# A decoder in one launch: the scan's C product made in place in SBUF, the state space's kernel spectrum moved to the shared lane, and new orders for all engines

## What is computed

```
x = LN(x + hawk(x))          # RMS norm, gated linear recurrence (RG-LRU), then a gated MLP
x = LN(x + cross_attention)  # 8 heads over a context of 32 positions
x = LN(x + mla + moe)        # latent causal attention, 16 heads; top-2 of 7 experts and a shared one
x = LN(x + selective_scan)   # below
x = LN(x + s4d_block)        # attention over x, FiLM, a state-space convolution by FFT, an MLP
x = LN(x + moe2)             # top-2 of 8 experts and shared ones
```

```
delta = softplus(x Wd + bd);  B = x Wb + bb;  C = x Wc + bc
h[n](t) = exp(delta(t) A[n]) * h[n](t-1) + delta(t) x(t) B[n](t)
y(t) = sum over n of h[n](t) * C[n](t)
```

## Time and profile before

| | us |
|---|---|
| median of 3 runs (lowest, highest) | 494.37 (493.97, 498.09) |
| span of the profiled execution | 494.8 |
| PE busy | 417.6 (84%) |
| DVE busy | 335.1 (68%) |
| ACT busy | 302.1 (61%) |
| POOL busy | 123.7 (25%) |
| 49 table loads on ACT | 62.9 |
| granted PE clock, mean | 0.934 of full speed |

### The profile page before, as it was taken

How to read it: one execution, slowest core, us unless ns; L and a number is a source line. 1 busy time by engine, 2 the same in 40 slices (tenths; PEclk the granted TensorE clock), 3 DMA queues, 4 the chain that set the end, 5 groups by cost and what they waited for, 6 DMA issues and landing times.

```text
span 494.8 us, 5930 instructions
## 1 busy us (share of the span) xinstructions
PE 417.6 (84%) x2049; PEld 203.1 (41%) x2049; DVE 335.1 (68%) x616; ACT 302.1 (61%) x513; POOL 123.7 (25%) x129
## 2 busy tenths in 40 slices
PE   6979868778979999978876874677699899999995
PEld 3535422353335554424332321425466644444442
DVE  2497776488877842745888997998965453554453
ACT  5648795514246679896788885554336687822443
POOL 1100460000420054058729484555020000000000
PEclk9999999959999999989996997668979999999999
DMA  7950000733280000023028778989300000000000
GB/s 266 338 168 15 1 2 0 200 54 148 70 186 5 3 3 1 3 63 108 0 69 208 190 177 229 212 228 273 157 0 1 1 0 1 0 1 0 1 21 21
DMA packets 23613, 42.39 MB, mean 86 GB/s; under 512 B 6965, under 2 KB 12310, under 8 KB 22422
## 3 DMA queue, kind: packets, MB, share of 16 engines
q1 hardware_dynamic: 23476, 41.92, 30.3%
q10 hardware_dynamic: 108, 0.10, 0.1%
HBM read 36.93 MB, written 4.98 MB: 85 GB/s over the span
## 4 chain that ended last, share of the span: by engine, by line
PE 55%; DVE 20%; ACT 8%; POOL 6%; issue 5%; DMA 5%; SPq 0%; DVEq 0%; ACTq 0%; POOLq 0%
DVE AR L1520 7%; PE PS L900 6%; PE PS L927 6%; PE PS L905 6%; ACT AR L1178 5%; PE PS L814 4%; PE PS L828 4%; DVE AR L1841 3%; POOL AR L2158 3%; PE PS L797 3%; PE PS L664 3%; DVE AR L1526 2%; DMA AR<-scan 2%; PE PS L1031 2%; DVE stats L1529 1%
## 5 line engine op out<-in xcount | busy, mean ns | idle before, releaser
L1178 ACT ACTIVATE AR<-PS 128x512 f32<-128x512 f32 (+2 forms) x185 | 98.4, 562 | 99.4 <-PE PS L900 44.2
L1520 DVE TENSOR_TENSOR AR<-PS,AR 128x512 f32<-128x512 f32 (+1 forms) x120 | 79.8, 678 | 57.6 <-PE PS L905 27.7
L2158 POOL TENSOR_TENSOR AR<-AR 128x512 f32<-128x512 f32 (+2 forms) x48 | 53.7, 1129 | 90.9 <-DVE AR L1520 60.0
L1178 ACT ACTIVATE AR<-AR 128x256 f32<-128x256 f32 (+3 forms) x110 | 46.9, 462 | 44.4 <-DVE AR L1520 28.6
L1174 ACT ACT_TABLE_LOAD x49 | 62.9, 1283 | 0.9
L1529 DVE TENSOR_REDUCE stats<-PS 128x1 f32<-128x128 f32 (+4 forms) x88 | 43.6, 525 | 11.5 <-PE PS L800 6.9
L1841 DVE TENSOR_TENSOR_SCAN AR<-PS,AR 128x512 f32<-128x512 f32 x32 | 38.9, 1214 | 2.2 <-ACT PS L1178 2.2
L797 PE MATMUL PS<-RR 97*128 97x512 bf16 (+3 forms) x128 | 31.9, 322 | 6.4 <-DVE stats L1529 3.3
L664 PE MATMUL PS<-AR,W_sq 128*128 128x256 f32 x88 | 26.6, 413 | 12.4 <-ACT AR L1178 7.9
L2244 POOL TENSOR_TENSOR RR<-KL,lags 128x512 f32<-128x512 f32 x24 | 26.6, 1146 | 40.0 <-PE PS L817 39.9
L814 PE MATMUL PS<-RR 100*128 100x512 bf16 (+3 forms) x128 | 29.9, 306 | 1.4 <-ACT AR L1178 1.1
(11 more groups left out here) (239 smaller groups left out, 726.4 us busy)
## 6 DMA issues: line engine op xcount, KB each, us to landing
AR<-scan SPq DMA_DIRECT2D x64, 256.0 KB, 4.1
RR<-in_ffn SPq DMA_DIRECT2D x1, 2688.0 KB, 10.9
RR<-in_ones SPq DMA_DIRECT2D x2, 832.0 KB
RR<-in_ones SPq DMA_DIRECT2D x2, 784.0 KB
RA<-in_moe SPq DMA_DIRECT2D x1, 1539.5 KB, 6.3
W_mla<-in_mla SPq DMA_DIRECT2D x1, 1504.0 KB, 15.4
W_late<-in_late SPq DMA_DIRECT2D x1, 1076.0 KB, 12.0
RA<-in_xa SPq DMA_DIRECT2D x1, 1056.0 KB, 7.7
```

The lines of the kernel that those rows point to most:

```text
L1178: nc.scalar.activation(out_, in_, func, bias=bias, scale=scale).then_inc(*done("act", *step))
L1520: nc.vector.tensor_tensor(out_, a, b_, op).then_inc(*done("dve", *step))
L2158: nc.gpsimd.tensor_tensor(out_, a, b_, op).then_inc(*done("pool", *step))
```

## The change

Three things.

1. ACT's `bC` writes C with its bias to an SBUF buffer, A13 (`shares`), not in place into PSUM bank 0. The scan writes straight into a ring of seven (`RING`), and `hc` multiplies there in place: its two inputs are now both in SBUF. The waits for PE's `yn` stand before every fourth `sc` from the eighth, not before `hc` from the seventh; the wait for the rows' way to DRAM before `sc5`.
2. `kf0`, `kf1`, `ko`, `ks` and `kd` are steps of lane w, in bank 0, before the fifth layer; `ks` and `kd` write in place. `kp1` waits for a's `bC` (C has left the bank) instead of `hc15`. In bank 0, `kf1` waits for `ko`.
3. All four turn tables and the table loads are new: 44 loads instead of 49 (in a's scan 10 instead of 8; from the second experts' first unit to the end 11 instead of 18). Of the parameter steps, `P1` of DVE moves from behind a's `hc1` to between `sc15` and `hc15`, `rQ1`, `qQ0` and `qQ1` from ahead of a's scan into it; POOL's `U1`, `U2` of the second half from ahead of a's `by0` to behind `by5`, `V1` from behind `by0` to behind `by9`, `Q1` from behind `by9` to behind `by15`. `ks` and `kd` stand at b's `hc9` and `sc10` instead of `hc13` to `hc15`.

```diff
--- before.py
+++ after.py
@@ -144,6 +144,8 @@
 
 SUMMED = 4
 
+RING = (14, 15, 0, 1, 12, 7, 8)
+
 AHEAD = {"dl": 3, "dx": 4}
 SPLIT = ["kk", "qq", "kr", "qr", "kl", "ql"]
 HALVES = (0, 1)
@@ -184,7 +186,7 @@
...
-        *_ln("ln4"), "lni.sq", "lni.l", "lni.r", "xb.e", "lni.g", "xb.a", "s0", "s1", "s2", "s3", "xit", "ko", "xo", *_ln("lnf"), *_halves("lnf.g"),
+        *_ln("ln4"), "lni.sq", "lni.l", "lni.r", "xb.e", "lni.g", "xb.a", "s0", "s1", "s2", "s3", "xit", "xo", *_ln("lnf"), *_halves("lnf.g"),
...
@@ -197,7 +199,7 @@
...
-        "xb.m", "xb.d", "lni.x", "xb.u", "xb.i", "xb.k", "xb.p", "lni.z", "xin", "ks", "kd", "bs", "bd", "xr", "xi", "yr", "yi", "ye", "yo",
+        "xb.m", "xb.d", "lni.x", "xb.u", "xb.i", "xb.k", "xb.p", "lni.z", "xin", "bs", "bd", "xr", "xi", "yr", "yi", "ye", "yo",
...
@@ -206,13 +208,13 @@
...
-            *[f"{n}{h}" for h in HALVES for n in ("s1", "s2", "sQ", "eP", "eQ", "kp")], "kl"],
+            *[f"{n}{h}" for h in HALVES for n in ("s1", "s2", "sQ", "eP", "eQ", "kp")], "kl", "ko"],
-            "ed.s", "ed.m"],
+            "ks", "kd", "ed.s", "ed.m"],
...
@@ -221,45 +223,46 @@
 
 TURNS = {
     "pe":
-        "a7 w1 a6 w2 a1 w1 a8 w1 a2 w2 a4 b2 a1 b2 a2 b3 a1 b1 a1 b2 a2 b1 a1 b1 a2 b9 a4 b2 a1 b6 a2 b1 a1 b1 "
...
+        "a9 w1 a4 w1 a1 w2 a2 w1 a1 w2 a5 b2 a2 b2 a5 b3 a2 b1 a2 b2 a2 b2 a1 b4 a2 b4 a1 b1 a2 b1 a1 b3 a1 b5 "
...
     "dve":
-        "w1 a1 w2 a2 w1 a6 w1 a1 w6 a4 w1 a2 w2 a1 w3 a3 w3 a1 w2 a1 w3 b1 w1 b1 w7 b3 w1 b3 a1 w1 a2 w1 a2 w1 "
...
+        "a2 w1 a6 w3 a1 w3 a1 w9 a1 w1 a3 w1 a2 w2 a2 w1 b1 w1 b1 a2 b2 w1 b1 a2 b1 w3 b2 w1 a2 w1 a3 w1 a4 w1 "
...
     "act":
-        "a2 w1 a3 w1 b1 a3 w1 a3 w2 b1 a2 w1 a17 b4 w1 a1 w2 a1 b2 a4 b2 a1 b1 a1 b5 a1 b1 a1 b2 a1 b3 a14 b1 "
...
+        "a6 w1 a1 w1 a3 w1 b1 a2 b1 a1 w3 a9 b1 a1 b2 a1 b1 a4 b2 a8 b2 a1 b2 a1 w1 b5 a2 b5 a15 b1 a1 b1 a1 b4 "
...
     "pool":
-        "w39 b6 w13 a1 w2 a1 w1 a9 w1 a4 b1 a2 b16 w1",
+        "w39 b6 w12 a1 w1 a6 w2 a4 w1 a5 b1 a1 w1 b16 w1",
 }
 
 
 
 TABLES = (
-    "3:log 12:gelu 15:exp 26:log 36:gelu 38:log 42:sin 49:log 53:gelu 55:exp 67:log 94:gelu 101:log "
...
+    "2:log 10:gelu 12:log 14:exp 26:log 42:gelu 46:log 50:gelu 52:exp 65:log 92:sin 94:gelu 102:log "
...
 
 
 def steps_of(engine, lane):
     if lane == "w":
         return STEPS_W[engine]
-    left_out = {("dve", 1): [*SPLIT, "ks", "kd"], ("act", 1): ["ko"], ("pool", 0): SPLIT,
+    left_out = {("dve", 1): SPLIT, ("pool", 0): SPLIT,
                 ("pe", 1): ["sp0", "sp1", "sp2"]}.get((engine, lane), ())
     return [n for n in STEPS[engine] if n not in left_out]
 
@@ -478,7 +481,10 @@
 
         def weighted(b, i):
 
-            return A(b, (0, 1, 12, 13, 7, 8)[i % 6])
+            return A(b, RING[i % len(RING)])
+
+        def shares(b):
+            return A(b, 13)
 
         def bank(i):
             return PS[:, i, :]
@@ -984,11 +990,6 @@
 
                 return x[:, HT * j + p:HT * j + HT:2]
 
-            def kernel_spectrum(c):
-
-                last = forward(own(0, 1 + c), 1 - c, KL)
-                last.then_inc(*done("pe", "w", f"kf{c}"))
-
             def state_space(b):
                 pe.wait_ge(*after("dve", b, "X4"))
                 for i in range(NT):
@@ -1004,7 +1005,7 @@
                 yield
                 pe.wait_ge(*after("act", b, "xb.a"))
                 if not b:
-                    pe.wait_ge(*after("act", "w", "kl"))
+                    pe.wait_ge(*after("dve", "w", "kd"))
                 for o in range(4):
                     mm(own(b, o), VF[:, b, 128 * o:128 * o + 128], A(b, 3), start=True, stop=True)\
                         .then_inc(*done("pe", b, f"fl{o}"))
@@ -1017,10 +1018,6 @@
                 yield
                 pe.wait_ge(*after("act", b, "xit"))
                 pe.wait_ge(loads["dft"], 16 * DFT_LOADS)
-                if not b:
-                    for c in range(2):
-                        kernel_spectrum(c)
-                        yield
                 for k, p in enumerate((1, 0)):
                     last = forward(own(b, (0, 3)[p]), p, XT[b])
                     last.then_inc(*done("pe", b, f"xf{k}"))
@@ -1138,7 +1135,7 @@
                     pe.wait_ge(*after("dve", "w", f"P{h}"))
                     pe.wait_ge(*after("pool", "w", f"Q{h}"))
                     if h:
-                        pe.wait_ge(*after("dve", 0, f"hc{NS - 1}"))
+                        pe.wait_ge(*after("act", 0, "bC"))
                     else:
                         pe.wait_ge(*after("dve", 0, f"hw{U0 - 1}"))
                     for i in range(16):
@@ -1154,6 +1151,11 @@
                     last = tr(own(0, 0)[:, 128 * j:128 * j + 128], every_second(Kdl, j // 2, j % 2), w("sq", "id"))
                 last.then_inc(*done("pe", "w", "kt"))
                 yield
+                pe.wait_ge(loads["dft"], 16 * DFT_LOADS)
+                for c in range(2):
+                    pe.wait_ge(*after("act", "w", ("kl", "ko")[c]))
+                    forward(own(0, 0), 1 - c, KL).then_inc(*done("pe", "w", f"kf{c}"))
+                    yield
 
             take_turns("pe", {"a": batch(0), "b": batch(1), "w": shared_program()})
 
@@ -1388,7 +1390,7 @@
                 f(A(b, 2), own(b, 3), ACT.Identity, (b, "bB"), bias=bB)
                 yield
                 act.wait_ge(*after("pe", b, "bC"))
-                f(own(b, 0), own(b, 0), ACT.Identity, (b, "bC"), bias=bC)
+                f(shares(b), own(b, 0), ACT.Identity, (b, "bC"), bias=bC)
                 yield
                 for i in range(NS):
                     act.wait_ge(*spread_of(b, "dl", i))
@@ -1430,10 +1432,6 @@
                 act.wait_ge(*after("pe", b, "xit"))
                 f(XT[b], grid(own(b, 2), 128), ACT.Copy, (b, "xit"))
                 yield
-                if not b:
-                    act.wait_ge(*after("pe", "w", "kf0"))
-                    f(Up[0][:, NF:2 * NF], own(0, 1), ACT.Copy, (b, "ko"))
-                    yield
                 act.wait_ge(*after("pe", b, "xf0"))
                 f(Up[b][:, 0:NF], own(b, 3), ACT.Copy, (b, "xo"))
                 yield
@@ -1509,6 +1507,10 @@
                     yield
                 act.wait_ge(*after("pe", "w", "kt"))
                 f(KL[:, :, :].rearrange("p j d -> p (j d)"), own(0, 0), ACT.Copy, ("w", "kl"))
+                yield
+                act.wait_ge(*after("pe", "w", "kf0"))
+                act.wait_ge(kdraft, 16 * 4)
+                f(Ksb[:, NF:2 * NF], own(0, 0), ACT.Copy, ("w", "ko"))
                 yield
 
             take_turns("act", {"a": batch(0), "b": batch(1), "w": shared_program()}, load_tables)
@@ -1838,18 +1840,18 @@
                 for i in range(NS):
                     dve.wait_ge(*after("act", b, f"aa{i}"))
                     dve.wait_ge(*after("pool", b, f"by{i}"))
-                    nc.vector.tensor_tensor_scan(A(b, 14 + i % 2), own(b, 1 + 2 * (i % 2)), scan_row(b, "dx", i), 0.0,
+                    if i == RING.index(7):
+                        dve.wait_ge(written["dx", b], 16)
+                        dve.wait_ge(written["dl", b], 16)
+                    if i >= len(RING) and not (i - len(RING)) % SUMMED:
+                        dve.wait_ge(*after("pe", b, f"yn{(i - len(RING)) // SUMMED}"))
+                    nc.vector.tensor_tensor_scan(weighted(b, i), own(b, 1 + 2 * (i % 2)), scan_row(b, "dx", i), 0.0,
                                                  ALU.mult, ALU.add).then_inc(*done("dve", b, f"sc{i}"))
                     yield
                     mine(b, f"sc{i}")
                     if not i:
                         dve.wait_ge(*after("act", b, "bC"))
-                    if i == 4:
-                        dve.wait_ge(written["dx", b], 16)
-                        dve.wait_ge(written["dl", b], 16)
-                    if i >= 6 and not (i - 6) % SUMMED:
-                        dve.wait_ge(*after("pe", b, f"yn{(i - 6) // SUMMED}"))
-                    tt(weighted(b, i), own(b, 0), A(b, 14 + i % 2), ALU.mult, (b, f"hc{i}"))
+                    tt(weighted(b, i), weighted(b, i), shares(b), ALU.mult, (b, f"hc{i}"))
                     yield
                 dve.wait_ge(*after("pe", b, f"yn{NS // SUMMED - 1}"))
                 for h, c in COLS:
@@ -1894,14 +1896,6 @@
 
                     return t.rearrange("p (s c n) -> p s c n", s=2, c=2)
 
-                if not b:
-                    dve.wait_ge(*after("pe", "w", "kf1"))
-                    dve.wait_ge(*after("act", b, "ko"))
-                    odd = Up[b][:, NF:2 * NF]
-                    butterfly(Ksb[:, 0:NF], own(0, 2), odd, ALU.add, "ks")
-                    yield
-                    butterfly(Ksb[:, NF:2 * NF], own(0, 2), odd, ALU.subtract, "kd")
-                    yield
                 dve.wait_ge(*after("pe", b, "xf1"))
                 dve.wait_ge(*after("act", b, "xo"))
                 odd = Up[b][:, 0:NF]
@@ -1911,7 +1905,7 @@
                 yield
```

(8 more changed lines are left out.)

## The result

The changed kernel takes 505.3 us in the median of four runs against 495.6 for the kernel before. The ratio on record is 1.0165, with a 95% interval of 1.012 to 1.021 (the two medians alone give 1.0195, inside it). That is 8.2 us more (5.9 to 10.4). It lies inside the range of 486 to 505 (502.5 by the ratio from 494.4), but it is not the "within 1%" that was forecast as likeliest. The nearest of the forecast's cases is rival 1, with 503.1. The profiled execution has a span of 500.8 us, 6.0 more than that of before. All ratios leave out the executions that count as slow, those more than 1.5% above the fastest of their kernel: none here, one each of e3, e6, e8 and e9, and four of e1's ten, of which three at about 500 us would bring e1's ratio from 0.995 to 0.999.

The account below looks back on a forecast made before the run. DVE was taken to bound both scans, PE the stretches 143.2 to 248.1 and 357.5 to 490.9 us. The terms 0 − 4 + 0 + 7 + 1 − 1 − 0.5 = +2.5 gave a 496.9 us median, range 486 to 505.

Parts of the forecast that it names:

- within 1%: Whole kernel: the forecast's likeliest outcome, a median between 489.5 and 499.3 us, chance 0.43.
- rival 1: Both scans: delays from the lock add up, nothing is absorbed; +13.2 replaces +7, giving 503.1 us; chance 0.21.
- The mechanism of the product: Both scans: a product with two SBUF inputs waits for POOL's running instruction, ending about 0.55 us after it.
- the other 4.2 can absorb. That leaves +7: Both scans: 10.9 us of product delays, partly absorbed by 4.2 us of DVE idle time: +7 (0 to +13.2).
- rival 2: Both scans: DVE and POOL alternate, the lock costs 1 us or less; 487.0 or 490.9 us; chance 0.25.
- the lock: Both scans: DVE operations with two SBUF inputs and POOL operations reading SBUF exclude each other; forecast at +7.
- K's steps in a's scan: a's scan: ACT's added operations and table loads can make an `aa` late, +1 us (0 to +3).
- rival 3: a's scan: ACT becomes the bound, making it 5 us longer instead of 1; 501 us; chance 0.11.
- 0, −4 and 0: Up to 248.1 us: first stage 0 (±3), 98.5 to 143.2 us −4 (−7.9 to 0), then 0 (±3).
- `ed.s` −1.0: Ahead of the tail: this 2.01 us reduction no longer stands ahead of `X4`, at most 2.0, taken as −1 us.
- Seven fewer table loads on an ACT that is idle for 61.4 us: −0.5: Tail: seven fewer loads on ACT and PE's 4.7 idle us give −0.5 us (−2 to +1).
- The signs that were named: Changed profile: products over 1 us beside POOL, scans +7 together, b's maxima 4 earlier, last stage within 1 of 133.4.

Follow-up runs that it names:

- e3: The changed kernel with C left in PSUM for batch b alone, a's products still in SBUF: ratio 1.0038 to the kernel before.
- e6: The kernel before with the new order in the tail alone, but `ed.s` back ahead of b's `X4`: ratio 0.9951 to the kernel before.
- e8: The kernel before with the new order in the tail alone, plus seven superfluous table loads on ACT: ratio 0.9993 to the kernel before.
- e9: The kernel before with new front and tail, and b's first two scans and products ahead of a's `s4` on DVE: ratio 0.9929.
- e1: The changed kernel with C kept in PSUM, so products read one PSUM input; ring and orders as changed: ratio 0.9953 to the kernel before.
- e2: The kernel before with C in SBUF, the ring of seven and the product in place, but its own orders: ratio 1.0160, 7.9 us.
- e4: The changed kernel with C in PSUM and the old order up to the end of a's scan: ratio 0.9937 to the kernel before.
- e5: The kernel before with the new order in the tail alone, 11 table loads there instead of 18: ratio 0.9916, −4.2 us.
- e7: The kernel before with the new order in front and tail, the middle with both scans as before: ratio 0.9902 to the kernel before.

## Why the prediction came out as it did

**The mechanism of the product: right, its size in this order: too small.** The forecast said that a product with both inputs in SBUF waits for POOL's running instruction and ends about 0.55 us after it. The changed kernel and e2 show that for all 35 products that had more than 0.14 us of it to wait for. The overlay on the trace of before gave 10.9 us; measured were 10.4 and 12.2. What came out too small is the next step, "the other 4.2 can absorb. That leaves +7". It holds for the old order (e2: +7.9, 4 us absorbed). In the new one the product costs 10.6 us (changed against e1; 10.2 of 10.4 in the two scans), so next to nothing was absorbed. DVE had idle time enough for it, 2.3 us in e1's scan of a and 3.8 in b's. But of b's, 1.58 us (for an `aa`) and 0.86 (for ACT) stand behind b's first scans and are as long in the changed kernel as in e1, and in a's scan the idle time is 2.9 us in the changed kernel and so did not shrink. Why the old order's idle time shrank and this one's didn't is not shown further.

**Rival 1: near, in part by luck.** It said that nothing is absorbed, which is what the new order did. It also put the lock at 13.2 us, by the whole product following POOL's end; the products end 0.55 us after it, and the lock costs 10.6. Its 503.1 is close to 502.5 because the errors nearly cancel: against its sum the product is 2.6 cheaper, the front with K's steps 3.8 dearer, b's scan 1.0 dearer and the tail 2.7 cheaper (below).

**Falling into step (rival 2): no.** 18 and 21 of the 32 products start inside a POOL instruction. POOL is busy 0.67 of a's scan and 0.45 of b's in the changed kernel, which gives 18 by chance.

**K's steps in a's scan: the size about right, the reason not.** "+1 (0 to +3)" came from ACT. ACT held up nothing there: rival 3 is out, since no wait for an `aa` is left in a's scan. But K's own operations took 4.3 us in e1's scan and 3.2 ahead of it in the kernel before, beside POOL's instructions in the first case; and `Q1` behind `by15` made b's first scan wait for POOL, which no term had. The run ratios give only sums: e1 against e4 is the front, K's steps and the hand-over together, +0.8 us; with the front at −0.1 to −0.7 this leaves +0.9 to +1.5 for the rest, against +1, all with an uncertainty of 2 us.

**b's scan: no term.** The forecast had the new order of b's scan at nothing. e4 against e5 puts it at +1.0 by the runs, again with 2 us of uncertainty, and at +3.4 by hand-over and scan of the profiles (44.69 against 41.28 us), where DVE waits 4.3 us in e4's scan of b and 0.9 in e5's.

**`kp1` does come where it came before**, behind `hc15`, as forecast: at 316.5 us.

**The front: the step that missed by most, beside the product.** The terms were 0, −4 and 0 for the stages up to 248.1. Over the five profiles with the new front and the six with the old one, a's maxima start 2.8 us later (102.2 against 99.4), b's 2.3 earlier (141.4 against 143.7, not 4), and b's scores 2.6 earlier; a's scan begins only 0.1 us earlier (e7 and e9). So what the second stage gained was lost again between b's scores and a's scan, for which the forecast had no loss, and −4 came out as −0.1 to −0.7. The forecast also misread where b's cross-attention stood: two of its four pairs of products (96.02 and 96.64 us) were already ahead of a's maxima in the kernel before, and 99.66 is the third.

**The tail: the sign right, the size a third.** `ed.s` −1.0 is −1.7 (e6); from the kernel before to e5 it is −1.1, since the new order also puts the second half of a product of a (0.6 us) ahead of `X4`. "Seven fewer table loads on an ACT that is idle for 61.4 us: −0.5" is −2.0 in the profile and more in the runs (e8). An average of idle time was no cover; what fits is that a load stands between PE's product and the activation that PE's next product waits for, though no single such wait was followed. The tail's first ten us also differ by the granted clock: 0.66 in the profile of before, 0.83 in the changed kernel's, 1.00 in e1's. At 0.83 the old tail takes 136.5 us (e2), the old number of loads in the new order 134.9 (e8) and the new tail 132.85 (e5). So the loads are 2.0 of 3.6 us at an equal clock, the other 1.6 is the rest of the order, which no run takes apart, and the kernel before's 137.3, at 0.66, is 0.8 above that of e2.

**The signs that were named.** Products of over 1 us beside POOL and of 0.69 without, DVE the busiest, `kp1` behind `yn3`: seen. The two scans' stages are 13.0 and 4.4 us longer, not 7 together; b's maxima are 2.3 us earlier, not 4; the last stage is 4.3 us from 133.4, not within 1. The first stage moved by 3.1 us in the one pair of profiles, 2.8 in the means, so the forecast's own sign of being wrong there (more than 3) was met or just missed.

Sum, by the runs: product +10.6, front with K's steps and the hand-over +0.8, b's scan +1.0, tail −4.2: +8.2, against +2.5 forecast. The product (+3.6) and the steps up to the hand-over (forecast −4 + 1 = −3, so +3.8) made the difference, b's scan added 1, and the tail, −2.7 on its forecast, hid part of it. That the total stayed inside the range owes to this last error: without it, it would be 505.2.

In the earlier trace rows the POOL product of 1.82 us is listed from 334.94 us, 0.02 ahead of DVE's, and yet it was POOL that waited: between starts this close the list doesn't tell which of the two went first.

By the Trainium skill ("ScalarE: Activation LUTs", section "What ACT_TABLE_LOAD costs") a switch of tables has a drain of 1.38 us behind its 1.28 us. The changed kernel's trace disagrees: its 44 loads, which do switch, are of 1283 ns each, and behind nearly all of them the next operation starts 0.01 us later, as in the kernel before. The measurement decides.

## What to carry to other kernels

Before moving an operand from PSUM to SBUF, look at who else is at work: lay the new operations over POOL's instructions on the old timeline, count those that meet one, and price each at the rest of it; that came within 12% twice. Don't take an average of idle time off the sum: here 4 us were absorbed in one order and next to nothing in another with as much idle time. Follow a gain to the next stage that everyone waits for: the front's 2.6 us were gone by the start of a's scan. And an engine that is idle for about half of a stage can still be on the path in it, as ACT's seven loads were in the tail.

## What was not expected of the hardware

The wait goes both ways, and it adds up: POOL's `by` products took 1.66 to 1.72 us instead of 1.27 in eight cases in the changed kernel, after a DVE operation had started first or had just been let in, and the four pieces of `Q1` took 6.97 us added up instead of 5.10. It is not the products' alone either: of K's operations on DVE a tensor-scalar of 128 x 1024 took 1.26 us in e1's scan instead of 0.75.

With the same order the time to b's `su0` still varied from 177.8 to 183.1 us between executions, and from 140 to 160 us the granted clock was 1.00 in the kernel before and 0.74 in e5. Differences of 1% in this kernel need ten runs, not one profile.
